# Deformable convolution and a gated feed-forward: the taps of two of four images made with source pixels on partitions

## The reference

```python
ys = py + kh + off_y
xs = px + kw + off_x
sampled = _bilinear_sample(x, ys, xs)
sampled = sampled * mask[:, None]
w = w_dcn.reshape(w_dcn.shape[0], C, KK)
return jnp.einsum('bckhw,ock->bohw', sampled, w)
```

## Time and profile before

| what | us |
| --- | --- |
| median of 3 runs | 108.91 |
| lowest, highest | 108.62, 109.21 |
| the profiled execution | 108.63 |
| its span, first to last instruction | 106.8 |
| PE busy, share of the span | 97.6, 91% |
| DVE busy | 69.3, 65% |
| ACT busy | 50.7, 47% |
| DMA moved | 2.37 MB |

### The profile page before, as it was taken

The page is one execution under the profiler, slowest core; times in us unless marked ns, Lnnn a source line. Parts: engine busy times, 40 slices in busy tenths (PEclk is TensorE's granted clock), DMA queues, the critical chain, the costliest instruction groups (busy, mean ns, idle before and its releaser), DMA issues.

```text
span 106.8 us, 1840 instructions
## 1 busy us (share of the span) xinstructions
PE 97.6 (91%) x624; PEld 53.4 (50%) x624; DVE 69.3 (65%) x196; ACT 50.7 (47%) x99; POOL 13.9 (13%) x25
## 2 busy tenths in 40 slices
PE   4946899989998989999999999999999999999990
...
DVE  4599999999998999876664495253255932205241
...
PEclk9999999999999999999999999999999999999999
...
DMA packets 1976, 2.37 MB, mean 22 GB/s; under 512 B 816, under 2 KB 1456, under 8 KB 1968
## 3 DMA queue, kind: packets, MB, share of 16 engines
...
...
## 4 chain that ended last, share of the span: by engine, by line
PE 73%; DVE 13%; issue 6%; ACT 3%; DMA 2%; POOL 1%; DVEq 0%; POOLq 0%
PE taps_ps L674 16%; PE bank_y L746 14%; PE bank_o L688 14%; PE hid_ps L734 9%; PE taps_ps L734 6%; ACT a_sb L350 2%; DMA xt<-in_x_tok 2%; PE hid_ps L661 2%; DVE a_sb L568 2%; PE bank_p L711 2%; DVE xn L529 2%; PE bank_c L724 2%; DVE at L460 2%; PE bank_p L696 1%; PE bank_p L724 1%
## 5 line engine op out<-in xcount | busy, mean ns | idle before, releaser
L674 PE MATMUL taps_ps<-ident,at 128*128 128x128 f32 x144 | 22.5, 283 | 1.6 <-ACT a_sb L350 1.0
L674 PEld LDWEIGHTS taps_ps<-ident,at 128*128 128x128 f32 x144 | 15.5, 142 | 11.0 <-issue 5.0
L460 DVE TENSOR_TENSOR at<-haty,hats 128x768 f32<-128x768 f32 x22 | 20.6, 951 | 0.1
L688 PE MATMUL bank_o<-a_sb,v_sb 128*64 128x256 f32 x144 | 18.1, 386 | 0.6 <-DVE a_sb L568 0.4
L350 ACT ACTIVATE a_sb<-taps_ps 128x512 f32<-128x512 f32 x22 | 12.9, 592 | 7.8 <-PE taps_ps L674 7.8
L382 ACT ACTIVATE hid<-hid_ps,b_col 128x512 f32<-128x512 f32 x20 | 13.1, 682 | 7.3 <-PE hid_ps L734 7.3
L746 PE MATMUL bank_y<-hid,w_sb 128*64 128x512 f32 x64 | 15.4, 604 | 0.0
L594 DVE SCALAR_TENSOR_TENSOR tmp<-bank_y,b_col,spread 128x512 f32<-128x512 f32 x8 | 6.0, 750 | 13.4 <-PE bank_y L746 13.4
L266 POOL TENSOR_TENSOR rs<-ve,power 128x2 f32<-128x2 f32 (+1 forms) x6 | 5.5, 916 | 65.6 <-DVE ve L475 61.4
L688 PEld LDWEIGHTS bank_o<-a_sb,v_sb 128*64 128x64 f32 x144 | 9.8, 136 | 7.1 <-issue 3.2
L568 DVE COPY a_sb<-taps_ps 128x512 f32<-128x512 f32 x14 | 9.5, 686 | 3.0 <-PE taps_ps L674 2.9
...
## 6 DMA issues: line engine op xcount, KB each, us to landing
w_sb<-in_w SPq DMA_DIRECT2D x2, 512.0 KB, 4.1
...
out<-fin SPq DMA_DIRECT2D x2, 128.0 KB, 1.8
...
```

The costliest lines, as they stand in the source:

```text
L460: dve.tensor_tensor(at[:, u % AT_RING, j, :, :].rearrange("p k (y x) -> p k y x", x=W), haty[:, b % 2, j, k0:k0 + GROUP, :].unsqueeze(3).b ...
L674: last = pe.transpose(t_bank(step)[:, st * HW + j * P:st * HW + (j + 1) * P], at[:, u % AT_RING, j, k, st * P:(st + 1) * P], ident[:, :])
L688: last = pe.matmul(bank_o[st * O:(st + 1) * O, 0:HW], v_sb[:, img, st, k, :], a_sb[:, slot % A_RING, st, :], start=(k == 0), stop=(k == TA ...
```

## The change

Images 0 and 1 keep the old path. For images 2 and 3 (`DIRECT = 2`) the 256 x 256 matrices are made at once with source pixels on partitions. PE turns the hats themselves instead of the taps: step `hT` transposes the 8 first taps' y and x hats (four transposes of 128 columns, `hT.0`) and those of the ninth tap (four of 16 columns, `hT.1`). Step `hs` copies them out of PSUM (`hs.0` 128 x 512 on ACT, `hs.1` 16 x 512 on DVE). SP writes them with three DMAs (two of 128 KB, one of 32 KB) to the scratch `hat_rows` in HBM, waits until all three have landed, and reads them back with three DMAs for each unit, each 128 partitions x 3 KB: the x hats with each of 16 source rows repeated for 8 partitions, and for either half of the y hats 8 source rows, the whole set repeated 16 times. So each partition, which is one source pixel, receives the y hat of its row and the x hat of its column for 256 output pixels of three taps. Step `pd` (one DVE instruction for each unit, 128 x 1536) multiplies them straight into three slots of `a_sb`. `M` of these images waits for `pd`. Steps `pr`, `T` and `E` of slots 18 to 35 are gone: 12 DVE products, 18 x 4 PE transposes, 12 copies on ACT and 6 on DVE.

`spread_hats` has one copy for all: the reads for a unit of image 3 wait for `pd` of the same taps of image 2. `v_sb` of images 2 and 3 holds its source pixels in the order column, row (`sources`, `pixels`). To make room, `adist`, `haty`, `xn2`, `fin` and half of `ya` are gone; results are written in place, `at` has 3 parts instead of 4, `hats` 3 instead of 2, and `dist` of an image now waits for `relu` of the one before it. All four order tables and the bank table are new.

```diff
+DIRECT, HAT_RING = 2, 3
+AT_RING, A_RING, H_RING = 3, 9, 3
...
-    "xnT0 conv0 V0.1 omT0 xnT1 V0.0 conv1 V1.1 omT1 T0 xnT2 T1 xnT3 T2 V1.0 M0 T3 T4 conv2 conv3 T5 omT2 T6 T7 V3.0 T8 omT3 T9 M1 "
+    "xnT0 V0.1 conv0 V0.0 omT0 xnT1 xnT2 conv1 V1.0 omT1 conv2 T0 xnT3 T1 omT2 T2 conv3 M0 hT2.1 hT2.0 T3 V1.1 T4 T5 V3.1 T6 omT3 "
...
-        adist = sb("adist", [P, NT, 2 * TAPS, W])
-        hats = sb("hats", [P, 2, NT, 2 * TAPS, W])
-        haty = sb("haty", [P, 2, NT, TAPS, W])
+        hats = sb("hats", [P, HAT_RING, NT, 2 * TAPS, W])
+        hrow = sb("hrow", [P, 2, HW])
+        hrow_last = sb("hrow_last", [W, 2, HW])
+        spread_hats = sb("spread_hats", [P, 1 + ST, TAPS, HW])
...
+        rows = nc.dram_tensor("hat_rows", (NB - DIRECT, 2, W, TAPS, HW), F32).ap()
+
+        def sources(b):
+
+
+            return xflat[:, b, :] if b < DIRECT else xflat[:, b, :].rearrange("p (s x y) -> p s x y", s=ST, x=W)
+
+        def pixels(b):
+            flat = misc(f"xnT{b}")[:, 0:HW]
+            return flat if b < DIRECT else flat.rearrange("p (s y x) -> p s x y", s=ST, x=W)
...
+            for b in range(DIRECT, NB):
+                i = b - DIRECT
+                sp.wait_ge(*saved(hrow_saved, f"hs{b}.0"))
+                for c in range(2):
+                    sp.dma_start(rows[i, c, :, 0:TAPS - 1, :].rearrange("x k t -> k x t"), hrow[:, c, :]).then_inc(rows_written[i], 16)
+                sp.wait_ge(*saved(hrow_saved, f"hs{b}.1"))
+                sp.dma_start(rows[i, :, :, TAPS - 1, :].rearrange("c x t -> x c t"), hrow_last[:, :, :]).then_inc(rows_written[i], 16)
+                sp.wait_ge(rows_written[i], 48)
+                for g in range(UNITS):
+                    u = UNITS * b + g
+                    if i > 0:
+                        sp.wait_ge(tap_made, upto(f"pd{u - UNITS}"))
+                    taps = slice(GROUP * g, GROUP * g + GROUP)
+                    flat = rows[i, :, :, taps, :].rearrange("c x k t -> c x (k t)")
+                    shape = [W, RPT, GROUP * HW]
+                    there = hats_spread[u - UNITS * DIRECT]
+                    sp.dma_start(spread_hats[:, 0, taps, :], flat[1].unsqueeze(1).broadcast_to(shape)).then_inc(there, 16)
+                    for s in range(ST):
+                        down = flat[0, s * RPT:(s + 1) * RPT].unsqueeze(0).broadcast_to(shape)
+                        sp.dma_start(spread_hats[:, 1 + s, taps, :], down).then_inc(there, 16)
...
-                    act.activation(adist[:, :, :, :], dist[:, :, :, :], ACT.Abs).then_inc(abs_done, 1)
+                    act.activation(dist[:, :, :, :], dist[:, :, :, :], ACT.Abs).then_inc(abs_done, 1)
...
+                elif kind == "hs":
+                    act.wait_ge(hatT, upto(f"hT{b}.{n[1]}"))
+                    if b > DIRECT:
+                        act.wait_ge(rows_written[b - DIRECT - 1], 48)
+                    if n[1] == 0:
+                        act.activation(hrow[:, 0:2, :].rearrange("p c t -> p (c t)"), misc(f"hT{b}.0")[:, :],
+                                       ACT.Copy).then_inc(hrow_saved["ACT"], 1)
+                    else:
+                        act.activation(hrow_last[:, :, :].rearrange("x c t -> x (c t)"), misc(f"hT{b}.1")[0:W, :], ACT.Copy).then_inc(hrow_saved["ACT"], 1)
...
-                    dve.wait_ge(abs_done, upto(f"abs{b - 1}"))
+                    dve.wait_ge(relu_done, upto(f"relu{b - 1}"))
...
+            def spread_product(u):
+
+
+                k0 = GROUP * (u % UNITS)
+                slot = GROUP * u
+                dve.wait_ge(hats_spread[u - UNITS * DIRECT], 16 * (1 + ST))
+                dve.wait_ge(unit_mm, (slot + GROUP - 1 - A_RING) // GROUP + 1)
+                dve.tensor_tensor(
+                    a_sb[:, slot % A_RING:slot % A_RING + GROUP, :, :],
+                    spread_hats[:, 1:, k0:k0 + GROUP, :].rearrange("p s k t -> p k s t"),
+                    spread_hats[:, 0, k0:k0 + GROUP, :].unsqueeze(2).broadcast_to([P, GROUP, ST, HW]), ALU.mult).then_inc(tap_made, 1)
...
+                elif kind == "hT":
+                    take(BANK[step], saved(hrow_saved, f"hs{b}.{n[1]}"))
+                    pe.wait_ge(haty_ready, upto(f"haty{b}"))
+                    first, m = (0, P) if n[1] == 0 else (TAPS - 1, W)
+                    for c in range(2):
+                        for j in range(NT):
+                            flat = hats[:, b % HAT_RING, j, c * TAPS:(c + 1) * TAPS, :].rearrange("p k x -> p (k x)")
+                            last = pe.transpose(misc(step)[0:m, c * HW + j * P:c * HW + (j + 1) * P], flat[:, first * W:first * W + m], ident[:, :])
+                    last.then_inc(hatT, 1)
...
-                    for slot in range(GROUP * b, GROUP * b + GROUP):
-                        pe.wait_ge(*saved(tap_saved, f"E{slot}"))
+                    if img < DIRECT:
+                        for slot in range(GROUP * b, GROUP * b + GROUP):
+                            pe.wait_ge(*saved(tap_saved, f"E{slot}"))
+                    else:
+                        pe.wait_ge(tap_made, upto(f"pd{b}"))
```

More of the change, by code:

```diff
@@ L64 @@
 HOMES = {
-    'c': (
-        "xnT0 omT0 conv1 xnT2 conv2 omT2 xT0 wdT0 sp0.1 sp0.2 sp0.3 sp1.1 sp1.3 Fa0 "
-    ),
     'p': (
-        "conv0 xnT1 omT1 xnT3 conv3 omT3 oT0 oT1 xT1 gate0 oT2 sp0.0 xT2 oT3 xT3 gate1 wdT1 sp1.0 sp1.2 Fa1 "
+        "xnT0 conv0 xnT1 conv1 omT1 xnT3 conv3 hT2.1 omT3 oT0 oT1 xT0 gate0 wdT0 sp0.1 sp0.0 oT3 sp0.3 wdT1 sp1.3 sp1.2 "
+        "Fa0 "
     ),
     'h': (
-        "V0.1 V0.0 V1.1 V1.0 V3.0 V2.1 V2.0 V3.1 H0.0.0 H0.0.1 H0.1.0 H0.1.1 H0.2.1 H0.3.1 H1.0.0 H1.1.0 H1.2.0 H1.3.0 "
+        "V0.1 V0.0 V1.0 V1.1 V3.1 V2.1 V2.0 V3.0 H0.0.0 H0.1.0 H0.2.0 H0.3.0 H0.3.1 H1.0.1 H1.1.1 H1.2.1 H1.3.1 "
+    ),
+    'c': (
+        "omT0 xnT2 conv2 omT2 hT2.0 hT3.0 hT3.1 xT1 oT2 sp0.2 xT2 xT3 gate1 sp1.0 sp1.1 Fa1 "
     ),
     1: (
-        "T0 T2 T3 T5 T6 T9 T10 T12 T16 T18 T20 T22 T24 T28 T29 T31 T33 T35 "
+        "T0 T2 T4 T8 T11 T12 T14 T16 "
     ),
     0: (
-        "T1 T4 T7 T8 T11 T13 T14 T15 T17 T19 T21 T23 T25 T26 T27 T30 T32 T34 "
+        "T1 T3 T5 T6 T7 T9 T10 T13 T15 T17 "
     ),
     't': (
-        "H0.2.0 H0.3.0 H1.0.1 H1.1.1 H1.2.1 H1.3.1 "
+        "H0.0.1 H0.1.1 H0.2.1 H1.0.0 H1.1.0 H1.2.0 H1.3.0 "
     ),
@@ L176, in metaformer_kernel @@
         rs2 = sb("rs2", [P, NB, NT])
-        xn2 = sb("xn2", [P, NB, NT, 2, C])
         x2s = sb("x2s", [P, NB, HW])
```

64 lines of the change are left out of this document (38 added, 26 removed), and 26 rows, old and new, of tables (ACT_ORDER, DVE_ORDER, PE_ORDER).

## The result

| | us | runs |
| --- | --- | --- |
| kernel before | 108.95 (108.62 to 109.21) | 4 |
| changed kernel | 105.68 (104.16 to 108.86) | 4 |
| ratio | 0.961 (0.952 to 0.971) | |
| predicted | 102.0 (98.8 to 111.0) | |

The ratio says 3.9% faster, the two medians of the table 3.0% (105.68 of 108.95). The executions of the changed kernel differ by more than those of before, and they sort by the granted clock of TensorE: 104.16 us at a mean of 1.000, 105.24, 105.77 and 106.12 at 0.984, and 108.86 at 0.936. The last is the profiled one; that of 105.77 is a fifth one, not in the table's four.

A forecast was written before the change was run, and what follows sets the result against it. PE and DVE were taken to bound together up to about 48 us, then PE alone. 108.63 - 8.3 + 0.6 + 1.2 - 0.3 = 101.8 us profiled, 102.1 beside the median; forecast 102.0, range 98.8 to 111.0.

The forecast's parts named there:

- PE's own work: On PE: 18 `T` of 0.59 us removed, `hT` of two images added at 2.3 us; net -8.3 us.
- The front: Up to the end of `M0`: it ends at 21.4 us, 2.2 later, partly offset by work already done; net +0.6 us.
- The middle: From `M0` to `M8`: 31.3 us of PE work, waits of 2.1 us where 0.9 were; net +1.2 us.
- the two named places: PE's waits in the middle: 0.5 us for `pr5.1` ahead of `T15`, 0.3 for `lna1` ahead of `xT1`.
- rival B: DVE holds the middle, through `pd` at 2.3 us, new handoffs and late `abs2`; 104.3 to 105.5 us, chance 0.12.
- `pd`: DVE's product of 1536 elements takes 1.74 us by the slope; six take 10.4 us.
- The DMAs: Spread reads at 350 GB/s, 3.4 us a unit, lie beside other work and cost nothing.
- the slack of 6.2 us a unit: Spread reads: a unit may take 6.2 us (190 GB/s) before `M11` waits.
- rival A: Repeated source rows slow the spread reads, so `M11` is delayed and the kernel may be slower than before; chance 0.27.
- The end: After `M8`: about 0.3 us of waits for copies go along with the last eight `T`; net -0.3 us.
- C: The walk is too slow, in `M0` and PE's middle waits; 99.4 or 98.5 us; under 98.8 us, chance 0.06.
- the forecast's own range: Whole kernel, 98.8 to 104.3 us around 102.0, without the rivals; chance 0.55.

The follow-up runs named there:

- the profile with distinct reads: Changed kernel with all 18 spread reads taking 128 different expert-weight rows instead of repeated scratch rows; 104.05 us at full clock.
- E0: Not a run: a kernel step, a copy on ACT in the front.
- E13: Not a run: a kernel step, a copy on DVE in the changed kernel.
- The kernel with all three edits: Changed kernel plus 14 spare matmuls in PE's front gaps, `ya0.1` after `lna3`, and three steps moved from DVE to ACT; median 102.03 us, ratio 0.936.

## Why the prediction was near, and where it was wrong

The forecast for a profiled execution, 101.8 us, is held against the profile with distinct reads: full clock, same order of work, 104.05 us. So 2.2 us are missing there, and the clock takes the rest. By stages they split so:

| stage | forecast us | measured us | off |
| --- | --- | --- | --- |
| to the end of `M0` | 21.4 | 22.2 | +0.8 |
| from there to the end of `M8` | 33.4 | 33.3 | -0.1 |
| from there to PE's last matmul | 42.5 | 44.0 | +1.5 |
| behind it | 4.5 | 4.6 | +0.1 |

**PE's own work: right in kind, a little too large.** 72 `T` and 16 `hT` stand in the list, PE busy 89.8 us where about 89 was said. Eight groups of transposes put back cost 4.0 to 4.2 us, so the term was a real one. But 0.59 us for a `T` is the top of what the timeline of before shows: the last eight take 0.49 to 0.59 from their start to that of the next step, 4.3 us in all and not 4.7. Image 2's two `hT` take 0.44 and 0.43 and not 0.54 and 0.59, which goes the other way.

**The front: +0.6 was too little.** `M0` ended at 22.2 and not 21.4. The walk took `xn1` and `xn2` at the price of before; beside POOL's `sel0` they took 1.57 us, and 1.11 when it was moved. It took ACT's row as free for `E0`, and PE waited 0.93 for it ahead of `T2`. That these two make up the 0.8 was not shown: with both removed other waits came up, and the time stayed.

**The middle: the total right by two errors.** Waits of PE up to `M8` came to 2.9 us where 2.1 were said, and the two named places were off most: `T15` 1.48 where 0.5 was said, `xT1` 0.48 where 0.3 was. PE's work in the stage came to 30.4 us where 31.3 were said; some 0.4 of that are the cheaper `hT`. The two cancel, and `M8` ended 0.7 us late only because `M0` did: that this stage agrees is luck. The step ahead of `T15` was misread as well: it was to wait for the product `pr5.1`, and it waited for the copy `E13`, which stands behind that product on DVE and ended 0.6 us later. This is rival B's engine and place, not its causes: `pd` took 1.75 us and not 2.3, and of the 1 to 2 us for handoffs and a late `abs2` there was one wait of DVE for ACT's `abs2`, 0.36 us. That moving three steps gave 1.6 to 1.8 us shows that both waits were nearly full price.

**`pd`: right.** 1.74 us by the slope, 1749 ns measured.

**The DMAs: the rate was mis-sized, the conclusion held.** 350 GB/s was said, and 250 it was: 4.7 us a unit, not 3.4. A read's issue took 0.60 us and not 0.43. Three writes and their landing took longer too: the first read was issued at 27.8 us at full clock, not 26.5. All this fits in the slack of 6.2 us a unit, and the `pd` waited 0.0 us. The prediction looked for that slack at `M11`; DVE's own was smaller, at `pd9`, 0.02 us in the profiled execution and 0.67 in the second profile of the changed kernel. The prediction took the nearer row, a queue of distinct rows, for a source that repeats, and left 1.3 us a unit out of its sum; had the slack been 1 us a unit, it would have been wrong. By rival A's own formula, 6u - 40.9, a unit of 4.7 us gives no delay. The 103 GB/s of the Trainium skill's page "DMA: Bandwidth & Descriptors", section "Latency and other measured facts", is no measure of these reads: the page's case is a row pitch, and the rate here was 2.4 times that. The sense of its rule, streams in step on the same memory lose rate, fits with 250 against 400 GB/s, but no run here varied the pitch or tells where the rate is lost.

**The end: a gain of 0.3 was said, a loss came.** From `M8` on, the kernel before and the changed one do the same steps on PE but for the last eight `T`, so the stage can be compared row by row: 47.6 us before, 44.0 now, 3.7 less where the sum had 5.0. The eight `T` gave 4.3 and not 4.7. Waits of 0.25 and 0.26 us for copies went, as said. New ones of 0.93 came: 0.77 ahead of `xT3`, by POOL's `ya0.1`, and 0.16 ahead of `xT2`. Some 0.2 us stay unnamed. The prediction looked at DVE and the DMAs for new waits and never at POOL, whose sum had now moved beside `lna3`; before, it ran at 79.78 us, 4 us behind the square root that releases `lna3`.

**The clock: not considered at all.** The prediction read 1.00 all along and took that as given, though the change moved `xnT`, `conv` and `V` of the front and so split its gaps, from 1.38, 0.92 and 0.35 us to 1.03, 0.34, 0.72 and 0.59, and, by `lna3`, made one of 0.77 near the end. The kernel before had such gaps and dropped in 5 of 33 executions, so the reading of 1.00 in one profile was itself too little to rest on. The drops cost 1.1 to 2.2 us in most executions and 4.7 in the profiled one, against 103.96 to 104.16 at full clock. Of the 3.7 us between 102.0 and the median of 105.68 some 1.6 are the clock, and some 2.1 the terms above.

**The rivals.** A didn't come: 250 GB/s, no `pd` waiting. B came in part. C didn't. The median of 105.68 us lies above the forecast's own range, 98.8 to 104.3, and is inside the whole range because that was stretched to 111.0 for A and B: what it was widened for isn't what came, so that the range held is in part luck. At full clock, 103.96 to 104.16, the kernel lies in the forecast's own range. What no case held, the clock, moved the profiled execution more than any term of the sum but PE's.

The kernel with all three edits stands at 102.0 as well, but that doesn't bear the prediction out: it has waits removed that the prediction allowed for.
